# A cross attention whose value products come in three blocks per group instead of seven

## The reference, cut to what matters

```python
q = (x @ w_q).reshape(B, SQ, 16, 64)        # x: 2048 x 256
k = (cond @ w_k).reshape(B, SKV, 16, 64)    # cond: 1601 x 192
v = (cond @ w_v).reshape(B, SKV, 16, 64)
attn = einsum('bqhd,bkhd->bhqk', q, k) * 64 ** -0.5
attn = softmax(attn, axis=-1)
out = einsum('bhqk,bkhd->bqhd', attn, v).reshape(B, SQ, 1024)
return out @ w_out + b_out
```

## Time and profile before

| what | us |
|---|---|
| median of three runs (3599.75 to 3606.65) | 3599.84 |
| profiled execution | 3592.38 |
| its span, first to last instruction | 3590.6 |
| PE busy in the span | 3201.4 (89%) |
| DVE busy | 2355.7 (66%) |
| ACT busy | 1721.9 (48%) |
| POOL busy | 1711.3 (48%) |

### The profile page before, as it was taken

The page is one execution under the profiler, slowest core; times in us unless marked ns, Lnnn a source line. Parts: engine busy times, 40 slices in busy tenths (PEclk is TensorE's granted clock), DMA queues, the critical chain, the costliest instruction groups (busy, mean ns, idle before and its releaser), DMA issues. The chain is left out here.

```text
span 3590.6 us, 60640 instructions
## 1 busy us (share of the span) xinstructions
PE 3201.4 (89%) x22601; PEld 1809.7 (50%) x22601; DVE 2355.7 (66%) x5271; ACT 1721.9 (48%) x2086; POOL 1711.3 (48%) x1145
## 2 busy tenths in 40 slices
PE   6899999989999999999999817689979989999787
PEld 3666666644555555555555407655544333333346
DVE  3999999945656656656656481264427878888528
ACT  1788888833444344444344322222224656666641
POOL 2888888824767777777778702212350000000012
PEclk9999999999999999999999958889977999999999
DMA  2000000020000000000000066500021111111001
GB/s 71 25 2 2 2 2 2 2 53 1 4 1 3 4 1 4 1 4 1 4 1 1 1 197 202 151 13 1 1 42 17 17 17 17 17 17 17 18 14 36
DMA packets 62572, 88.14 MB, mean 25 GB/s; under 512 B 9458, under 2 KB 52339, under 8 KB 61427
## 3 DMA queue, kind: packets, MB, share of 16 engines
q1 hardware_dynamic: 59250, 80.27, 9.2%
q0 software_dynamic: 3072, 4.34, 0.7%
HBM read 61.28 MB, written 8.54 MB: 19 GB/s over the span
## 5 line engine op out<-in xcount | busy, mean ns | idle before, releaser
L921 DVE TENSOR_REDUCE x0hm<-x0pM 128x1 f32<-128x400 f32 (+1 forms) x1024 | 520.2, 561 | 379.7 <-PE x0pM L823 379.7
L402 POOL TENSOR_SCALAR rows<-rows,mb 128x1024 bf16<-128x1024 bf16 x512 | 567.4, 1119 | 131.2 <-DVE mb L354 131.2
L348 DVE TENSOR_SCALAR_CACHE_REDUCE rows<-pS 128x1024 bf16<-128x1024 f32 x512 | 616.4, 1205 | 19.0 <-PE pS L297 19.0
L413 ACT ACTIVATE prT<-pP 128x1024 bf16<-128x1024 bf16 x512 | 523.3, 1024 | 134.4 <-PE pP L308 133.9
L1381 DVE TENSOR_REDUCE x1hm<-x1pM 128x1 f32<-128x400 f32 (+1 forms) x1024 | 512.6, 564 | 112.3 <-PE x1pM L1273 112.2
L1500 ACT ACTIVATE x1pr<-x1pST 128x1024 f32<-128x1024 f32 (+1 forms) x416 | 419.2, 1023 | 218.3 <-PE x1pST L1325 208.1
L783 POOL TENSOR_TENSOR x0acc<-x0acc,x0pr 128x1024 f32<-128x1024 f32 (+1 forms) x176 | 421.4, 2395 | 111.1 <-ACT x0pr L1032 95.3
L783 POOL TENSOR_TENSOR x0acc<-x0acc,o_nat 128x1024 f32<-128x1024 f32 (+1 forms) x176 | 418.9, 2380 | 71.9 <-ACT o_nat L1032 53.1
L1273 PE MATMUL x1pM<-x1sk,x1sq 64*128 64x400 f32 (+1 forms) x1024 | 361.2, 451 | 58.4 <-DVE x1hm L1381 29.4
L2590 POOL MEMSET f_tri<- 128x128 f32 x1 | 0.2, 209 | 730.2 <-POOLq L1179 730.2
L1032 ACT ACTIVATE o_nat<-x0pST 128x1024 f32<-128x1024 f32 (+1 forms) x208 | 213.0, 1024 | 279.8 <-PE x0pST L867 279.6
(11 more groups left out here) (362 smaller groups left out, 5127.2 us busy)
## 6 DMA issues: line engine op xcount, KB each, us to landing
m_w<-in_moe_w1T SPq DMA_DIRECT2D x16, 1024.0 KB, 9.8
m_w<-in_moe_w2T SPq DMA_DIRECT2D x16, 1024.0 KB, 6.3
x1sq<-x1qh SPq DMA_DIRECT2D x32, 128.0 KB, 4.4
x1sk<-x1kh SPq DMA_DIRECT2D x32, 100.1 KB, 3.6
rows_d<-m_xr SPq DMA_DIRECT2D x1, 2176.0 KB, 7.8
acc_d<-m_zero SPq DMA_DIRECT2D x4, 514.0 KB, 7.4
m_acc<-acc_d SPq DMA_DIRECT2D x4, 514.0 KB, 6.8
g_xN<-in_x SPq DMA_DIRECT2D x1, 2048.0 KB, 8.8
```

The source lines that it names most:

```text
L348: nc.vector.tensor_scalar(rows[u][:, half * 1024:(half + 1) * 1024], pS[half][:, :], 1.0, None, ALU.mult, ALU.max, accum_out=mx[u][:, half ...
L402: nc.gpsimd.tensor_scalar(r, r, -1.0, mb[u][:, 0:1], ALU.mult, ALU.add).then_inc(s_df, 1)
L413: nc.scalar.activation(prT[u][:, half * 8:(half + 1) * 8, :], pP[half][:, :, :], ACT.Exp, scale=-1.0 / HD ** 0.5).then_inc(s_ex, 1)
L921: emptied(nc.vector.tensor_reduce(hm[g % 2][:, a, t, i % 8 // 2:i % 8 // 2 + 1], bank(name)[:, 0:w], AX.X, ALU.max, negate=True), name)
```

## The change

The values come in three blocks: after the units of step 4 (the values of steps 0 to 3), of step 8 (4 to 7) and of step 0 of the next group (8 to 12). There are six places for exponentials. The units over the full array stand in front of these three blocks: sum and q at step 4, both k at step 8, both halves of out at step 0. The places of the units "max" and "shift", and of the reciprocals (steps 5 to 8) and the normalising (step 9) on VectorE, stay. To make room, the output is copied straight into `on` and normalised there, the denominators are inverted in place, and `unit_rows` becomes the tile of ones that exists already (only the rows 0 and 64 of `sh` are not zero), with three memsets less.

```diff
-    NP = 4
+    NP = 6
@@ units_in
-        if kt == 1 and g + 2 < GROUPS:
+        if kt == 0 and g >= 2:
+            units += [("out", g - 2, 0), ("out", g - 2, 1)]
+        if kt == 4 and g >= 1:
+            units.append(("sum", g - 1))
+        if kt == 4 and g + 2 < GROUPS:
             units.append(("q", g + 2))
-        if kt == 3 and g >= 1:
-            units.append(("sum", g - 1))
-        if kt == 11 and g >= 1:
-            units.append(("out", g - 1, 0))
-        if kt == 0 and g >= 2:
-            units.append(("out", g - 2, 1))
-        if g // 4 + 1 < H // 2 and g % 4 < 2 and kt in (5, 9):
-            units.append(("k", g // 4 + 1, 2 * (g % 4) + kt // 9))
+        if kt == 8 and g // 4 + 1 < H // 2 and g % 4 < 2:
+            units += [("k", g // 4 + 1, 2 * (g % 4)), ("k", g // 4 + 1, 2 * (g % 4) + 1)]
         return units
+    def values_in(n):
+        kt = n % NK
+        if kt in (4, 8):
+            return range(n - 4, n)
+        return range(n - 5, n) if n and kt == 0 else ()
...
-        unit_rows = m.sb("x0unit", [P, P], F32R)
+        unit_rows = G.ones[:, :].bitcast(F32R)
...
-                    if kt == 1:
-                        values(n - 1)
-                    elif n and kt % 2 == 1 or n and kt == 0:
-                        values(n - 2)
-                        values(n - 1)
-                values(STEPS - 2)
-                values(STEPS - 1)
+                    for k in values_in(n):
+                        values(k)
+                for k in values_in(STEPS):
+                    values(k)
@@ reciprocals, normalise (DVE)
-                    if i == 0 and g >= 1:
-                        dve.wait_ge(s_on, g)
-                    nc.vector.reciprocal(rc[:, c], dn[:, c]).then_inc(s_rc, 1)
+                    nc.vector.reciprocal(dn[:, c], dn[:, c]).then_inc(s_rc, 1)
-                    if g >= 2:
-                        wait_filled(dve, ("out", g - 2, 1))
-                    nc.vector.tensor_tensor(on[g % 2][:, :], oc[:, :], rc[:, :], ALU.mult).then_inc(s_on, 1)
+                    nc.vector.tensor_tensor(on[g % 2][:, :], on[g % 2][:, :], dn[:, :], ALU.mult).then_inc(s_on, 1)
@@ sums, copy_out (ACT)
                     if g >= 1:
-                        act.wait_ge(s_rc, 4 * g)
+                        act.wait_ge(s_on, g)
                     act.wait_ge(s_pv, NK * (g + 1))
-                    if g >= 1:
-                        act.wait_ge(s_on, g)
-                    nc.scalar.activation(oc[:, :], pO[:, :], ACT.Copy).then_inc(s_oc, 1)
+                    if g >= 2:
+                        wait_filled(act, ("out", g - 2, 1))
+                    nc.scalar.activation(on[g % 2][:, :], pO[:, :], ACT.Copy).then_inc(s_oc, 1)
```

More of the change, by code:

```diff
@@ L659, in l0_cross_heads @@
     number, count = {}, 0
-    last = [("out", GROUPS - 2, 1), ("sum", GROUPS - 1), ("out", GROUPS - 1, 0), ("out", GROUPS - 1, 1)]
+    last = [("out", GROUPS - 2, 0), ("out", GROUPS - 2, 1), ("sum", GROUPS - 1), ("out", GROUPS - 1, 0), ("out", GROUPS - 1, 1)]
     for name in first + [n for g in range(GROUPS) for kt in range(NK) for n in units_in(g, kt)] + last:
@@ L676, in l0_cross_heads @@
         sh = [m.sb(f"x0sh{i}", [P, QG], F32R) for i in range(2)]
-        unit_rows = m.sb("x0unit", [P, P], F32R)
+        unit_rows = G.ones[:, :].bitcast(F32R)
         kept = G.o_nat[:, :, :].rearrange("p c n -> p (c n)").bitcast(F32).rearrange("p (b a q) -> p b a q", b=2, a=2)
-        pr = [kept[:, 0, :, :], kept[:, 1, :, :]] + [m.sb(f"x0pr{i}", [P, 2, QG])[:, :, :] for i in range(2)]
+        pr = [kept[:, 0, :, :], kept[:, 1, :, :]] + [m.sb(f"x0pr{i}", [P, 2, QG])[:, :, :] for i in range(NP - 2)]
         acc = [m.sb(f"x0acc{i}", [P, 2, QG]) for i in range(2)]
@@ L684, in l0_cross_heads @@
         dn = m.sb("x0dn", [P, QG])
-        rc = m.sb("x0rc", [P, QG])
-        oc = m.sb("x0oc", [P, QG])
         on = [m.sb(f"x0on{i}", [P, QG]) for i in range(2)]
@@ L749, in _ @@
                 sp.dma_start(wo[:, :, :], A["x0_wo"].rearrange("(j p) n -> p j n", p=P)).then_inc(s_wo, 16)
-                sp.wait_ge(s_set, 4)
+                sp.wait_ge(s_set, 2)
                 shift_rows(0)
@@ L761, in _ @@
                     nc.gpsimd.memset(sh[i][:, :].bitcast(F32), 0.0).then_inc(s_set, 1)
[L762 to L767, removed]
+                pool.wait_ge(s_set, 2)
                 pool.wait_ge(s_bo, 16)
@@ L884, in values @@
                     mm.then_inc(s_pv, 1)
-                pe_.wait_ge(s_set, 5)
+                pe_.wait_ge(s_set, 2)
                 for name in first:
@@ L991, in _ @@
                 unit(last[0])
+                unit(last[1])
                 for i in range(4):
@@ L994, in _ @@
                 normalise(GROUPS - 1)
-                for name in last[2:]:
+                for name in last[3:]:
                     unit(name)
```

## The result

The changed kernel takes **3777.5 us** (median of four runs, 3760.3 to 3778.6) against 3599.8; the ratio is 1.048, with a 95% interval of 1.0446 to 1.0514. Slower was forecast, but with 3627 us in a range up to 3655, so the size was far off.

A forecast was written before the change was run, and what follows sets the result against it. VectorE's reductions and reciprocals, not TensorE's work, were taken to set the pace. Groups 1 to 29 add 30.9 us, less 3.2 at the ends: +27.7 us, giving 3627 us, range 3592 to 3655.

The forecast's parts named there:

- VectorE, not TensorE, sets the pace between blocks: Between value blocks TensorE waits for VectorE's reductions and reciprocals; groups without k 1.2 us longer.
- The chain of steps 5 to 8: VectorE's reductions and three reciprocals in steps 5 to 8, without a gap, 6.50 us; TensorE waits 3 us there.
- the tenth maximum: TensorE's last maximum in steps 5 to 8 starts 8.04 us after the block ahead, three late.
- cycles 12.1 and 12.0 us: TensorE's times for steps 1 to 4 and steps 5 to 8, each with its block of four values.
- Storage, places and memsets at nothing: Output copied into `on`, in-place inverting, tile of ones, six places and fewer memsets: no change in time.
- The gain of a removed block: Fixed cost of a value block on TensorE, 0.3 to 0.4 us; four removed, 1.2 to 1.7 us a group.
- Six places and GpSimd's load: Exponentials never wait for a place; GpSimd's additions take 30.3 us of a 37.9 us group, leaving it idle.
- the normalising, put at 0.90 us with bounds 0.67 and 1.29: VectorE's normalising of the output at step 9, taken as 0.90 us when other work follows.
- Rival 4: TensorE's longer waits lower its clock in the stage to 0.88: about 156 us more, 3780 us; chance 0.02.
- Forecast for these groups were 30.9: Groups 1 to 29: 16 without k by 1.2 us and 13 with k by 0.9 us more.
- what the prediction called unknown: Interleaving of scores and late maxima, entry to full units, the normalising: 0.5 to 2.0 us more per group.
- time moved outside this stage: Sign that the forecast is wrong: time changing ahead of or behind the changed stage; no size given.

The follow-up runs named there:

- e4: The changed kernel with all four reciprocals at the end of step 4 and the normalising at the end of step 8; 3550.9 us, ratio 0.9849.
- e1: The changed kernel's storage (places, in-place work, tile of ones) with the order of the kernel before; 3606.9 us, ratio 0.9996.
- e7: e4 with its second value block cut in two, so one value block a group more; 3556.6 us, ratio 0.9881.
- e6_filler: The changed kernel with eight more pairs of score products in step 11 of each group but the first; 3756.4 us, ratio 1.0427.
- e5_shortadds: The changed kernel with GpSimd's additions of steps 2 to 12 cut to 64 of 512 queries; 3654.2 us, ratio 1.0141.
- e2_norm8: The changed kernel with the normalising at the end of step 8 instead of step 9; 3654.0 us, ratio 1.0114.
- e3_recips4: The changed kernel with all four reciprocals at the end of step 4 instead of in steps 5 to 8; 3597.3 us, ratio 0.9978.
- e8_fillers: The changed kernel with eight more pairs of score products in step 11 and six more in step 8; 3691.9 us, ratio 1.0246.

## Why the prediction was wrong

**Right, by its steps.** VectorE, not TensorE, sets the pace between blocks: shown by e4. The chain of steps 5 to 8: 6.50 us computed, 6.50 measured; the tenth maximum 8.04 us behind the block, computed and measured; cycles 12.1 and 12.0 us against 12.2 and 12.0. Storage, places and memsets at nothing: e1. The gain of a removed block: e7. Six places and GpSimd's load cost nothing by themselves.

**Wrong, first: the normalising, put at 0.90 us with bounds 0.67 and 1.29.** It took 2.88, outside its bounds; from its start to that of the next instruction, which is what the 0.90 stood for, 2.80. 1.90 us in 29 groups are 55 us. The bounds came from a phase in which most of GpSimd's addition was already over. The kernel before has the same wait, only short:

```profile
1129.22 4.89 POOL L783 TENSOR_TENSOR x0acc<-x0acc,x0pr 128x1024 f32<-128x1024 f32 x2
1133.69 0.97 DVE L950 TENSOR_TENSOR x0on<-x0oc,x0rc 128x512 f32<-128x512 f32 x1
1134.25 5.17 POOL L783 TENSOR_TENSOR x0acc<-x0acc,o_nat 128x1024 f32<-128x1024 f32 x2
```

The addition ends at 1134.11, 0.42 us into the normalising, and the normalising at 1134.66, again 0.55 behind, and the next pair of additions takes 5.17 us instead of 4.89. The spread of 669 to 1290 ns in one and the same instruction was the sign, and the window of the earlier trace rows left out the plainest case. Taken over the whole stage the trace of before has a normalising of 2369 ns, at 2004.89, half a microsecond into an addition:

```profile
L950 DVE TENSOR_TENSOR x0on<-x0oc,x0rc x32: 669/976/2369, 906.5 to 2057.7; 128x512 f32<-128x512 f32 x32
...
2004.33 2.38 POOL L783 TENSOR_TENSOR x0acc<-x0acc,o_nat 128x1024 f32<-128x1024 f32 x1 [0.41 <-ACT o_nat L1032]
...
2004.89 2.37 DVE L950 TENSOR_TENSOR x0on<-x0oc,x0rc 128x512 f32<-128x512 f32 x1
```

Here too it ends 0.55 us behind the addition. An estimate of the upper bound from these rows is a whole addition of 2.4 and 0.55 = 2.95 us. The Trainium skill (SBUF — State Buffer, Who interferes with whom) has it so: a VectorE instruction with two inputs in SBUF contends with a GpSimd instruction that reads SBUF, while its reductions never do. The traces agree with both halves, as far as they go: nearly all of the reductions here read PSUM. With the 2.4 us of an addition from the rows, the rule would have set the bound.

**Wrong, second: the clock, a rival with a chance of 0.02.** The argument was that short waits of before had left it at 1.00. Idle times of 1.9 us and those of steps 7 and 8 did not. The forecast had the latter in its own sum (3 us of waiting in steps 5 to 8) and still had nothing for the clock in it. The table counts, over groups 1 to 29 of each profiled execution, the falls of the granted clock, and gives TensorE's idle pieces of over 0.2 us.

| kernel | idle per group, us | longest piece, us | falls |
|---|---|---|---|
| before | none | none | 0 |
| changed | 3.6 | 1.92 | 40 |
| e6_filler | 1.7 | 0.85 | 22 |
| e5_shortadds | 1.7 | 0.85 | 17 |
| e2_norm8 | 1.7 | 0.85 | 11 |
| e3_recips4 | 0.9 | 1.91 | 8 |
| e8_fillers | 0.5 | 0.42 | 0 |
| e4_both | under 0.1 | 0.20 | 0 |

Why e6, e5 and e2 differ, with the same idle pieces, stays open. From the copy of group 0 to that of group 29 the changed kernel takes 1266.1 us and e8, in which the clock stays up although VectorE's chain is the same, 1196.7: the clock cost 69 us. Rival 4's 3780 us hit the total by chance: it had the clock at 0.88, where 0.93 was granted, and no longer normalising.

**The sum with measured terms.** From the copy of group 0 to that of group 29 the kernel before takes 1106.1 us, the changed one 160.0 more. Forecast for these groups were 30.9; 55 for the normalising and 69 for the clock make 155. The 5 us that are left are under 0.2 a group, within what the prediction called unknown. The two wrong terms are coupled: without the normalising in step 9 (e2) the low clock shrinks from 181 to 65 us as well.

**Outside the stage.** The prediction named time moved outside this stage as a sign of being wrong; 25 of the 186.2 us were. The 14.8 us at the start have nothing to do with the edit. VectorE's first instruction took 18.3 us, until 0.4 us after the last of a row of GpSimd memsets, as the timelines of the changed kernel show; in the profiled execution of before it took 1.35 us beside the same memsets.

```profile
5.37 18.77 DVE L172 TENSOR_SCALAR xc<-xp,cw 128x512 f32<-128x512 f32 x2 [5.37 <-DMA cw<-in_conv]
```

```profile
16.13 7.16 POOL L164 MEMSET kT<- 128x1024 f32 x8
```

It is there in e1, e2 and e3 too, and not in the profiled executions of before, e4, e5, e6, e7 and e8, so it comes and goes with the run. Steps of this size occur between the runs of one kernel (e4: 3541.3, 3541.8, 3560.0 and 3560.6 us); that they have this cause isn't shown, since only one execution of each kernel has a profile. Part of the 178 us between the medians may be of this kind. What follows the stage is the same code everywhere and took 1520 to 1539 us over the profiled executions (before 1527.9, changed 1538.1); no experiment was made on the 10.2 us between these two.

## What to carry to other kernels

When blocks of work are merged to save switches, list what the other engines did under each of the old blocks and move it under the new ones; here a gain of 1.5% became a loss of 4.8% for two placements. Where an instruction's duration varies in the trace without a change of shape, as the normalising's did from 0.67 to 2.37 us, look at what the neighbouring engine runs beside it, over the whole stage and not a part of it, and bound it by the neighbour's longest instruction. Price idle time of TensorE twice, once as it is and once in the clock behind it: here pieces of 0.6 to 0.85 us, once a group, were enough for some falls, and together with one of 1.9 us they cost 69 us.

## What the runs showed of the hardware

- A multiplication of two SBUF tiles on VectorE (128x512) ends 0.55 us after the GpSimd addition that it starts beside: it takes 0.955 us with one of 0.45, 2.875 with one of 2.37, and 0.69 alone (e2). Reductions out of PSUM are no slower beside additions than alone: at most 0.58 us each by the profile, 0.48 from start to start.
- VectorE's `tensor_scalar` from SBUF to SBUF (128x512, mostly 0.47 to 1.35 us) took 18.2 to 18.7 us in four of ten profiled executions, from beside one of GpSimd's memsets to the end of their row; the memsets, one after the other, seem never to have let it in.
- The clock fell 40 times in 29 groups of the changed kernel, which has an idle piece of 1.9 us and those of steps 7 and 8, and in e5 17 times with pieces of at most 0.85 us. In these groups it did not fall in the kernel before, in e4, nor in e8 with pieces of at most 0.42 us.
- Filling idle time with useless products made the stage 70 us shorter than without them, though TensorE does 28 matmuls more in a group (e8).
